# One slot fewer and one shared step later in the second expert layer of a two-layer transformer kernel

## The reference

```
logits = x @ router_w                          # 8 choices, but Er = 7 routed experts
probs = softmax(logits); top1_val, top1_idx = best of probs
mask = (top1_idx[None] == arange(7)[:, None])  # a token whose best choice is the 8th has no routed expert
routed = sum over e of mask[e] * ((x @ up[e]) * silu(x @ gate[e])) @ down[e]
shared = ((x @ shared_up) * silu(x @ shared_gate)) @ shared_down
return 2 * top1_val * routed + shared
```

## Time and profile before

| what | value |
|---|---|
| three runs, device time | 1010.07, 1011.62, 1012.82 us; median 1011.62 us |
| profiled execution, span from first to last instruction | 1020.2 us |
| PE busy | 939.7 us (92%) |
| DVE, ACT, POOL busy | 633.1, 554.9, 462.6 us |
| mean granted TensorE clock | 0.979 of full |
| chain that ended last | PE 71%, issue 14%, ACT 6%, DVE 5%, DMA 2% |

### The profile page before, as it was taken

The page is one execution under the profiler, slowest core; times in us unless marked ns, Lnnn a source line. Parts: engine busy times, 40 slices in busy tenths (PEclk is TensorE's granted clock), DMA queues, the critical chain, the costliest instruction groups (busy, mean ns, idle before and its releaser), DMA issues.

```text
span 1020.2 us, 21591 instructions
## 1 busy us (share of the span) xinstructions
PE 939.7 (92%) x7416; PEld 604.4 (59%) x7416; DVE 633.1 (62%) x2087; ACT 554.9 (54%) x1078; POOL 462.6 (45%) x698
## 2 busy tenths in 40 slices
PE   8999999999989989999994898889997999999996
PEld 3566777777654233334642886456664644499994
DVE  4789998999815966853642444567773653344444
ACT  6536767667657555565421554558775522255551
POOL 1146776777642946620064554344552044323331
PEclk9999999999999989999997999999999999999999
DMA  6700000000020000040012225100000010111115
GB/s 208 229 2 3 3 2 2 3 2 2 3 83 11 0 1 1 0 165 0 1 48 63 73 76 167 31 2 2 2 2 1 1 32 29 48 44 50 49 32 175
DMA packets 32601, 42.01 MB, mean 41 GB/s; under 512 B 6960, under 2 KB 26800, under 8 KB 31632
## 3 DMA queue, kind: packets, MB, share of 16 engines
q1 hardware_dynamic: 27952, 31.26, 9.8%
q0 software_dynamic: 4544, 9.38, 2.8%
HBM read 29.16 MB, written 16.66 MB: 45 GB/s over the span
## 4 chain that ended last, share of the span: by engine, by line
PE 71%; issue 14%; ACT 6%; DVE 5%; DMA 2%; POOL 1%; SPq 1%; DVEq 0%; POOLq 0%; ACTq 0%
PE PS L693 6%; PE PS L434 5%; PE PS L676 5%; PE PS L476 5%; PE PS L683 5%; PE PS L447 4%; PE PS L330 3%; PE PS L339 3%; PE PS L627 3%; PE PS L629 3%; PE PS L636 2%; PE PS L536 2%; PE PS L427 2%; PE PS L783 2%; PE PS L802 2%
## 5 line engine op out<-in xcount | busy, mean ns | idle before, releaser
L911 ACT ACTIVATE pw<-PS 128x384 f32<-128x384 f32 x256 | 111.6, 488 | 71.5 <-PE PS L456 68.9
L1588 POOL TENSOR_SCALAR_AFFINE_SELECT pw<-pw 128x256 f32<-128x256 f32 x256 | 105.1, 434 | 75.0 <-ACT pw L911 73.1
L1186 DVE CUSTOM_DVE_ANT_0 PS<-PS,above 128x256 f32<-128x256 f32 x256 | 115.9, 453 | 23.0 <-PE PS L427 22.8
L1654 POOL DMA_INDIRECT token_rows<-xnb,slot_in x78 | 75.0, 962 | 119.3 <-ACT xnb L1014 113.5
L1640 POOL TENSOR_TENSOR XS<-XS,N 128x512 f32<-128x512 f32 x64 | 81.2, 1292 | 55.2 <-DVE N L1264 34.6
L434 PE MATMUL PS<-kf,qm 32*128 32x256 f32 x512 | 103.6, 426 | 0.5 <-POOL qm L1597 0.5
L1440 DVE TENSOR_TENSOR rsb<-sqb,PS 128x256 f32<-128x256 f32 (+1 forms) x78 | 43.2, 554 | 95.8 <-PE PS L683 44.1
L1188 DVE CUSTOM_DVE_ANT_0 PS<-PS,above 128x128 f32<-128x128 f32 x256 | 84.7, 331 | 0.0
L1610 POOL TENSOR_SCALAR_AFFINE_SELECT pw<-pw 128x256 f32<-128x256 f32 x128 | 56.1, 472 | 60.7 <-ACT pw L1059 60.7
L1597 POOL TENSOR_SCALAR qm<-qs,qmask 128x256 f32<-128x256 f32 x64 | 59.7, 933 | 44.1 <-ACT kf L892 44.1
L997 ACT ACTIVATE sqb<-PS 128x512 f32<-128x512 f32 x48 | 28.7, 597 | 88.9 <-PE PS L627 81.0
(11 more groups left out here) (214 smaller groups left out, 2406.6 us busy)
## 6 DMA issues: line engine op xcount, KB each, us to landing
sorted_rows<-empty_rows_dram SPq DMA_DIRECT2D x2, 2535.0 KB, 14.6
slot_in<-sorted_rows SPq DMA_DIRECT2D x78, 65.0 KB
N<-token_rows SPq DMA_DIRECT2D x16, 256.0 KB, 4.7
X<-xT_dram SPq DMA_DIRECT2D x8, 256.0 KB, 5.7
ATT<-gate_dram SPq DMA_DIRECT2D x1, 2048.0 KB
XS<-down_dram SPq DMA_DIRECT2D x1, 2048.0 KB
H<-up_dram SPq DMA_DIRECT2D x1, 2048.0 KB
out_dram<-X SPq DMA_DIRECT2D x8, 256.0 KB, 3.8
```

The lines of the kernel that those rows point to most:

```text
L911: nc.scalar.activation(pw[:, w % 2, j + n, :], PS[:, A_PST + (2 * v + n) % 3, 0:3 * P], ACT.Exp).then_inc(a_p, 1)
L1186: nc.vector.tensor_tensor_reduce(x[:, 0:SEQ], x[:, 0:SEQ], above[:, :], 1.0, -3e38, ALU.add, ALU.max, mx[:, t // 8 % 2, 1, j, g:g + 1])
L1588: m = nc.gpsimd.affine_select(x[:, :, SEQ * k:SEQ * k + P], x[:, :, SEQ * k:SEQ * k + P], [[0, 2], [1, P]], ALU.is_ge, 0.0, base=0, channe ...
L1654: nc.gpsimd.indirect_dma_start(token_rows[l][:, :], bass.IndirectOffsetOnAxis(slot_in[:, r, D:D + 1].bitcast(mybir.dt.int32), 0), slot_out ...
```

## The change

In the second layer 38 slots are run instead of 39. The rows of the 39th slot can only be tokens without a routed expert or padding; they are no longer returned. So that those tokens still read zero, SP fills the first 4096 rows of `token_rows` of the second layer from the empty rows, by one transfer behind the two fills, and POOL waits for 48 instead of 32 on `r_fill`. Three shared steps of the second layer run behind the slots, not two, and their order on PE becomes in 29, in 30, out 29, in 31, out 30, out 31. In the first layer the number of slots, the number of late steps and their order stay as they are.

```diff
+SLOTS_AT = (SLOTS, SLOTS - 1)
-        LATE = 2
+        LATE_AT = (2, 3)
...
             for l in range(2):
                 sp.dma_start(sorted_rows[l][:, :], a["empty_rows"]).then_inc(r_fill, 16)
+            sp.dma_start(token_rows[1][0:TOK, :], a["empty_rows"][0:TOK, 0:D]).then_inc(r_fill, 16)
...
-                for k in range(SLOTS):
+                for k in range(SLOTS_AT[l]):
...
-                    sp.wait_ge(q["sent"][r], 16 * (l + 1) * LOADS[r])
+                    sp.wait_ge(q["sent"][r], 16 * sum(n[r] for n in LOADS_AT[:l + 1]))
...
-                early = NCH * NH - LATE
+                early = NCH * NH - LATE_AT[l]
...
-                for j in range(early, NCH * NH):
+                shared_in(early)
+                for j in range(early + 1, NCH * NH):
                     shared_in(j)
-                for j in range(early, NCH * NH):
-                    shared_out(j)
+                    shared_out(j - 1)
+                shared_out(NCH * NH - 1)
...
-                shared_next(NCH * NH - LATE - todo[0])
+                shared_next(NCH * NH - LATE_AT[l] - todo[0])
...
-                shared_next(LATE)
+                shared_next(LATE_AT[l])
...
-                pool.wait_ge(r_fill, 32)
+                pool.wait_ge(r_fill, 48)
```

More of the change, by code:

```diff
@@ L231, in adaln_kernel @@
                dict(l=1, E=E1, NH=HID1 // P, HID=HID1, up=up1, gate=gate1, down=down1, rw=rw1, cap=E1 - 1, ln=LN_MODB1)]
-        LOADS = [(SLOTS - r + RING - 1) // RING for r in range(RING)]
+        LOADS_AT = [[(n - r + RING - 1) // RING for r in range(RING)] for n in SLOTS_AT]
         def of_slot(l, k):
-            return 16 * (l * LOADS[k % RING] + k // RING + 1)
+            return 16 * (l * LOADS_AT[0][k % RING] + k // RING + 1)
         @block.sync
@@ L701, in moe @@
                 turn(1)
-                for k in range(SLOTS + 1):
-                    if k < SLOTS:
+                for k in range(SLOTS_AT[l] + 1):
+                    if k < SLOTS_AT[l]:
                         gate_up(k)
-                    if k + 1 < SLOTS:
+                    if k + 1 < SLOTS_AT[l]:
                         columns[k + 1] = first_column(k + 1)
-                    if k + 2 < SLOTS:
+                    if k + 2 < SLOTS_AT[l]:
                         turn(k + 2)
@@ L997, in shared_silu @@
                     nc.scalar.activation(sqb[:, j % 2, :], PS[:, j % 2, :], ACT.Silu).then_inc(q["s_silu"], 1)
-                for j in range(NCH * NH - LATE):
+                for j in range(NCH * NH - LATE_AT[l]):
                     shared_silu(j)
@@ L1029, in moe @@
                 fetch_gate(1, columns[1])
-                for k in range(SLOTS + 1):
-                    if k < SLOTS:
+                for k in range(SLOTS_AT[l] + 1):
+                    if k < SLOTS_AT[l]:
                         silu(k)
-                    if k + 2 < SLOTS:
+                    if k + 2 < SLOTS_AT[l]:
                         fetch_gate(k + 2, columns[k + 2])
-                    if k + 3 < SLOTS:
+                    if k + 3 < SLOTS_AT[l]:
                         columns[k + 3] = first_column(k + 3)
@@ L1038, in moe @@
                         weight(k - 1)
-                for j in range(NCH * NH - LATE, NCH * NH):
+                for j in range(NCH * NH - LATE_AT[l], NCH * NH):
                     shared_silu(j)
@@ L1644, in moe @@
                 pool.wait_ge(q["pos"], 1)
-                pool.wait_ge(r_fill, 32)
+                pool.wait_ge(r_fill, 48)
                 for n in range(TILES):
-                    pool.wait_ge(q["s_hidden"], n * 7 // 8 + 3 if l else min(n * 2 // 3 + 1, NCH * c["NH"] + 2 - LATE))
+                    pool.wait_ge(q["s_hidden"], n * 7 // 8 + 3 if l else min(n * 2 // 3 + 1, NCH * c["NH"] + 2 - LATE_AT[l]))
                     nc.gpsimd.indirect_dma_start(sorted_rows[l][:, :], bass.IndirectOffsetOnAxis(pos[:, n:n + 1], 0),
```

## The result

| where | before, median us (runs) | changed, median us (runs) | ratio, 95% interval |
|---|---|---|---|
| first measurement | 1012.22 (4) | 1005.58 (4) | 0.9929, 0.9900 to 0.9958 |
| e5, chip 4 | 1011.85 (25) | 1007.08 (12) | 0.9947, 0.9930 to 0.9964 |
| e9, chip 2 | 1023.33 (23) | 1018.87 (12) | 0.9961, 0.9939 to 0.9982 |
| e13, chip 12 | 1023.55 (23) | 1019.86 (12) | 0.9972, 0.9949 to 0.9994 |

The change is faster in all four measurements. The differences of the medians are 6.6, 4.8, 4.5 and 3.7 us. The first measurement rests on four runs each, three of the four before being the given ones; its chip is not on record.

What follows compares the result with a forecast made beforehand. PE was taken to bound the kernel up to the last slot, with DVE late at the front edge. From 1011.62 us, -2.79 - 1.51 + 2.57 - 0.34 - 0.70 - 0.3 = -3.1, +0.85 for the clock: 1009.4 us, range 1007.4 to 1011.6.

Steps and rivals of the forecast that it cites:

- The slot: Second layer's slots: one slot less on every engine, PE's being the one that counts, -2.79 us.
- The front edge: Start of second layer's slots: DVE's first weight copy follows the addition of chunk 6, -1.51 us, bounds 0 and -2.57.
- The rival that the start gains less: Start of second layer's slots: front term falls toward 0, 1010.0 us without a clock fall, 1011.7 with one; chance 0.14.
- One more shared step behind the slots: End of second layer: PE has one more shared step between the last slot and `turn_back`, +2.57 us.
- The rival of products exposed each time: End: added step's products exposed each time, 0.7 us twice, 1010.8 us; chance 0.08.
- DVE's two waits: End additions: DVE no longer waits for the first and third returned chunks, -0.34 and -0.70 us.
- The stores: End of kernel: the last store no longer meets a queue, -0.3 us, bounds 0 and -0.9.
- The zero transfer: SP's early transfer of 2.1 MB behind the fills: costs 0, with a bound of +1 us.
- The clock: PE's hole before second layer's slots: clock falls in half of executions, 1.7 us each, taken as +0.85 us.
- the one in which the clock holds: Hole before second layer's slots: clock stays full in nearly every run, 1008.5 us; chance 0.28.
- The slower one: First attention: zero transfer holds up instruction fetches or last constants, would need 6.1 us to end over 1014.7; chance 0.05.
- the step moved is worth almost nothing: Both edges of second layer's slots: what the moved step gains in front it gives back behind.

Runs made afterwards that it cites:

- e5: The changed kernel again, no edit, against the kernel before on chip 4: 1007.08 against 1011.85 us, ratio 0.9947.
- e9: The changed kernel again, no edit, against the kernel before on chip 2: 1018.87 us, ratio 0.9961.
- e13: The changed kernel again, no edit, against the kernel before on chip 12: 1019.86 us, ratio 0.9972.
- e2: Changed kernel with two late steps in the second layer (slot removed, zero transfer kept), against the kernel before: 1021.88 us, ratio 0.9973.
- e10: Kernel before, storing only the eighth output chunk; one profiled execution, no times to compare: 2.52 us from last addition to end.
- e4: Kernel before plus only the zero transfer and the wait for it, against the kernel before: 1026.52 us, ratio 1.0009.
- e7: Changed kernel with four late steps in the second layer instead of three, against the kernel before: 1011.39 us, ratio 0.9993.
- filled kernels: Changed kernel with one or two idle PE matmuls before the second layer's slots, against the kernel before: ratios 0.9941, 0.9944, 0.9945.
- e3: Changed kernel with 39 slots and no zero transfer, only the third late step, against the kernel before: 1023.95 us, ratio 0.9989.
- e6: Changed kernel with two idle PE matmuls before the second layer's slots, against the kernel before on chip 4: 1006.10 us, ratio 0.9941.
- e1: A second copy of the kernel before, no edit, against the kernel before on chip 3: 1025.29 against 1025.14 us, ratio 1.0003.
- e8: Changed kernel with one idle PE matmul before the second layer's slots, against the kernel before on chip 2: 1017.52 us, ratio 0.9944.
- e11: Changed kernel, storing only the eighth output chunk; one profiled execution, no times to compare: 2.54 us from last addition to end.
- e12: Changed kernel with one idle PE matmul before the second layer's slots, against the kernel before on chip 12: 1017.65 us, ratio 0.9945.

## Why the prediction was wrong, step by step

- **The slot, -2.79 us: right.** 104.97 to 102.18 us, and 2.8 us by e2's ratio.
- **The front edge, -1.51 us: right in mechanism, a little small.** DVE's chain behind the addition of chunk 6 sets it, and the slot load comes in time. It measured -1.82, since the first weight copy follows the addition after 1.96 us here, not 2.28. The rival that the start gains less fell with this.
- **One more shared step behind the slots, +2.57: right**, +2.73 measured. The rival of products exposed each time fell too.
- **DVE's two waits, -1.04: too small**, -1.43. Both waits are gone. What I had read wrongly is the rest of the row: not DVE paced it, as I wrote, but the loads. PE's transposes of the fourth to the seventh chunk waited for them, and DVE's pairs of additions follow these transposes. Without that, DVE's row goes at 7.51 / 18 = 0.417 us an addition, against 5.24 / 12 = 0.437 in the earlier trace rows: the missing 0.4 us.
- **The stores, -0.3, bounds 0 and -0.9: the step that failed with the most weight.** It measured -1.21, 0.9 us more than the term and beyond its bound. I took 2.9 us, the quickest of the *loads*, for the landing of a store without a queue. But that load was the first of its burst, with none of the burst ahead of it, and it took 2.8 to 2.9 us in the other profiles too: it says nothing of a store, which e10 shows to land after 2.0 us.
- **The zero transfer, 0: right** as far as e4 can tell.
- **The clock, +0.85: a guess that the profiles do not bear out.** I argued that the hole in PE's work makes the clock fall in half of the executions. In none of the six profiles of a kernel with three late steps and no filling did it; with one chance in two, six in a row would be 1 in 64. PE was busy 0.80, 0.34 and 0.21 us in the windows 875 to 878 of the changed kernel, 1.35 us in all where I had 0.8 to 1.2, and the clock stayed at 2.4 GHz:

```profile
875.00:876.00 1.00, 0.80 (x2) 0.00 (x0) 0.59 (x2) 0.86 (x2) 0.00 (x0) 1.00 0.22 48
876.00:877.00 1.00, 0.34 (x1) 0.14 (x1) 0.32 (x1) 0.00 (x0) 0.00 (x0) 1.00 0.60 133
877.00:878.00 1.00, 0.21 (x2) 0.24 (x3) 0.65 (x3) 0.00 (x0) 0.00 (x0) 1.00 0.59 141
```

With one step more the hole is larger, and there the clock did fall (e7). Nor was the changed kernel's clock lower than the one before had: the mean over the runs is 0.9793 against 0.9781 in e5, 0.9790 against 0.9777 in e9, 0.9778 against 0.9788 in e13. What stays open is whether it falls now and then in executions that were not profiled: the filled kernels' lower medians and higher clocks speak for it, six profiles against.

Without the term for the clock, and with the store at its measured size, the sum is -2.79 - 1.82 + 2.73 - 1.43 - 1.21 = -4.5 us (the forecast's full-clock sum was -3.1). That agrees with three of the four measurements (4.8, 4.5 and 3.7 us). The first gave 6.6 us from four runs each; its interval, 0.4% to 1.0%, just reaches 4.5 us. What lies between is not explained by any stage that the change touches. The clock may have part in it by chance: those four runs of the changed kernel have a mean of 0.981, the twelve of e5 one of 0.979. The sum by stages alone, 1011.62 - 4.5 = 1007.1 us, lies below the range already. Of the 2.3 us between forecast and stages the store makes 0.9, the clock 0.85, the additions 0.4, the front 0.3; the late step gives 0.2 back.

Of the rivals, the one in which the clock holds came nearest. Its 1008.5 us stand against 1007.1 us by the stages. The slower one, of 6.1 us for the zero transfer, is refuted by e4.

**The change and its parts.** The prediction said that the step moved is worth almost nothing. That was wrong as well: it is worth 1.8 us in its stages (e3). The gain itself lies in front. At the end, where I had the step cost more than the waits give back, it costs nothing: PE works 2.66 us longer while the returned rows come in, and DVE's additions and the last store are shorter by the same 2.66 us. It is worth that only once: the fourth step costs 3.5 us by the profile of e7, where PE waits for the slot load and no wait at the end is left to cover.

## What to carry to other kernels

Moving one unit of work from before a stage to behind it pays while each side still has a wait that ends on something else; here the front was held by DVE's index loads and the end by returned rows, and one step more found both used up. When the last stores of a kernel are priced, take the latency of a store that nothing is queued ahead of: the fastest one in a full burst is no bound (3.2 us before, 2.0 us alone). And where a term is a guess about the clock, look for a profile of a hole of that very size before giving it weight, and compare the mean clocks of all runs, not only their times.

## What the runs showed of the hardware

**The first layer's slots depend on the chip.** Nothing was changed there, yet DVE's 39 slot products span 55.0 us in the first profile of the changed kernel and 54.9, 56.1 and 54.9 us on chip 4 (e5, e6, e7), but 66.4 us in the given profile of the kernel before, 67.3, 66.3, 68.2 and 66.2 us in e1 to e4 on chip 3, 65.4 to 67.0 us in the four on chip 2 (e8 to e11) and 65.3 and 65.6 us on chip 12 (e12, e13). The changed and the unchanged kernel are alike in it. This makes up 11.4 of the 17.2 us between the two pages. The given times of 1012 us were probably not taken on the chip of the given page: in every recorded run the device time is some 2 us above the span, and e1, a copy, has 1023.47 us with a span of 1021.4 us.

The chain that ended last shows what happens, first of the kernel before (start, duration, what):

```profile
563.88 0.45 PE PS L683 x4
564.33 0.11 PE PS L667
564.43 1.14 PE PS L693 x4
565.57 0.09 DVE rsb L1440
```

and of the changed kernel, in its first profile:

```profile
563.37 0.45 PE PS L685 x4
563.82 0.11 PE PS L669
563.92 0.45 PE PS L695 x4
564.37 0.45 PE PS L678 x4
```

In the second, PE runs from group to group, 0.45 us each, 1.45 us for a slot. In the first, DVE and ACT are released only 1.14 us after a down group began, and PE then has to wait for them. In the waits of that stretch of the kernel before:

```profile
DVE rsb L1440 <- PE PS L693: 13.7, 8, 1.9
...
PE PS L667 <- DVE xnb L1446: 6.0, 11, 1.0
```

Neither row has a counterpart in the same stretch of the changed kernel's first profile (558 to 613 us). In the second layer, where a slot takes 2.79 us, the slots' stage is the same on every chip, 104.97 us with 39 slots and 102.18 us with 38. I do not know what delays these releases, and no experiment here was about it.
